# Routed experts in pairs and singles of 128 rows, one three-buffer ring for both weights, and two reordered attention loops

## What is computed

```python
scores = sigmoid(flat @ centroids.T) + bias          # 16 routed experts
vals, idx = top_k(scores, 4)                         # 4 of them for every row
gating = zeros_like(scores).at[rows, idx].set(vals); gating /= gating.sum(-1)
for w1, b1, w2, b2, g in routed experts:             # D 512, hidden 352 (padded to 384)
    acc += (relu(flat @ w1 + b1) @ w2 + b2) * g[:, None]
```

## Time and profile before

| what | value |
|---|---|
| runs | 2126.97 us median of 3 (2122.52 to 2127.93) |
| the profiled execution | 2123.35 us, its span 2121.6 us |
| PE, DVE, ACT, POOL busy | 85%, 58%, 40%, 49% |
| granted TensorE clock, mean | 0.92 |
| DMA, mean | 149 GB/s |

### The profile page before, as it was taken

How to read it: one execution, slowest core, us unless ns; L and a number is a source line. 1 busy time by engine, 2 the same in 40 slices (tenths; PEclk the granted TensorE clock), 3 DMA queues, 4 the chain that set the end, 5 groups by cost and what they waited for, 6 DMA issues and landing times. The chain is left out here.

```text
span 2121.6 us, 29604 instructions
## 1 busy us (share of the span) xinstructions
PE 1803.0 (85%) x10016; PEld 1475.2 (70%) x10016; DVE 1231.4 (58%) x1916; ACT 848.3 (40%) x1426; POOL 1032.3 (49%) x654
## 2 busy tenths in 40 slices
PE   3389999999999688986669956765999999996996
PEld 2189999999999333432238845655999999995775
DVE  5244544444444579999606623662666666565886
ACT  3233333433333246455321211442666666661221
POOL 0325453545454245554312566213877777764564
PEclk7699999999999899998879977877999999998998
DMA  5634232323333400221680141103788778776564
GB/s 204 213 115 135 90 120 101 109 100 119 104 110 124 175 20 26 94 90 59 208 314 1 41 169 29 47 1 109 269 284 286 276 281 282 274 258 206 195 205 132
DMA packets 106858, 316.86 MB, mean 149 GB/s; under 512 B 14531, under 2 KB 16161, under 8 KB 105505
## 3 DMA queue, kind: packets, MB, share of 16 engines
q1 hardware_dynamic: 89536, 266.07, 36.5%
q0 software_dynamic: 17248, 49.86, 7.0%
HBM read 248.17 MB, written 67.71 MB: 149 GB/s over the span
## 5 line engine op out<-in xcount | busy, mean ns | idle before, releaser
L703 DVE TENSOR_TENSOR rffn_ps_h<-rffn_ps_hidden,rffn_silu 128x256 f32<-128x256 f32 x128 | 55.4, 432 | 234.3 <-ACT rffn_silu L658 234.3
L692 DVE TENSOR_TENSOR rows<-rffn_ps_y,rows 128x512 f32<-128x512 f32 x255 | 165.1, 681 | 2.5 <-PE rffn_ps_y L766 1.1
L745 PE MATMUL rffn_ps_hidden<-rffn_xsh,rffn_w0h 128*128 128x256 f32 x512 | 147.7, 288 | 0.0
L745 PE MATMUL rffn_ps_hidden<-rffn_xsl,rffn_w0h 128*128 128x256 f32 x512 | 146.0, 285 | 0.0
L745 PE MATMUL rffn_ps_hidden<-rffn_xsh,rffn_w0l 128*128 128x256 f32 x512 | 145.9, 285 | 0.0
L658 ACT ACTIVATE rffn_silu<-rffn_ps_hidden 128x256 f32<-128x256 f32 x144 | 53.3, 370 | 230.0 <-PE rffn_ps_hidden L745 226.6
L621 POOL TENSOR_TENSOR rffn_w0l<-rffn_raw,rffn_w0h 128x1536 fp32r<-128x1536 f32 x15 | 52.7, 3513 | 177.6 <-ACT rffn_w0h L642 177.6
L1873 POOL DMA_INDIRECT moe_x_in<-xn_rows,moe_idx_now x94 | 99.4, 1057 | 21.2 <-issue 14.7
L1879 POOL TENSOR_TENSOR moe_w_0l<-moe_raw,moe_w_0h 128x1536 fp32r<-128x1536 f32 x24 | 84.3, 3514 | 40.2 <-ACT moe_w_0h L1904 40.2
L745 PEld LDWEIGHTS rffn_ps_hidden<-rffn_xsh,rffn_w0h 128*128 128x128 f32 x512 | 99.2, 194 | 3.6 <-issue 0.3
L745 PEld LDWEIGHTS rffn_ps_hidden<-rffn_xsl,rffn_w0h 128*128 128x128 f32 x512 | 99.3, 194 | 1.8
(11 more groups left out here) (710 smaller groups left out, 6352.5 us busy)
## 6 DMA issues: line engine op xcount, KB each, us to landing
rffn_raw<-in_ffn_w SPq DMA_DIRECT2D x80, 768.0 KB, 4.3
moe_raw<-in_moe_w SPq DMA_DIRECT2D x47, 769.5 KB, 4.3
moe_raw<-in_moe_w SPq DMA_DIRECT2D x47, 768.0 KB, 5.2
ys<-moe_y SPq DMA_DIRECT2D x47, 512.0 KB, 3.0
xs<-route_zero SPq DMA_DIRECT2D x17, 256.0 KB
rffn_x_in<-xs SPq DMA_DIRECT2D x17, 256.0 KB, 2.7
ys<-rows SPq DMA_DIRECT2D x17, 256.0 KB, 2.1
rows<-in_x SPq DMA_DIRECT2D x4, 1024.0 KB, 9.0
```

The costliest lines, as they stand in the source:

```text
L692: nc.vector.tensor_tensor(y[:, 2 * u + tt, :], yb[n % 2][tt][:], y[:, 2 * u + tt, :], ALU.add)\
L703: nc.vector.tensor_tensor(hp[:, n % 2, :], hb[n % 2][:, 1, :], sil[n % 2][:], ALU.mult)\
L745: last = nc.tensor.matmul(hb[n % 2][:, half, :], wu[p][:, col:col + P], xs[q][:, c, u * PR:(u + 1) * PR], start=(c == 0 and m == 0), stop= ...
```

## The change

The routed experts' rows are now padded to 128, not 256. Every expert has full tiles of 256 rows (a pair of 128) and, where 128 rows or fewer are left, a single of 128. There are `MP` = 31 pairs and `MS` = 17 singles, 48 units in place of 47 tiles, in the fixed order 2, 2, 1, fourteen times, then 2, 1, three times; the units of a kind take the experts' rows in turn, and `places` and `shares` compute the places and experts of both kinds. A single does the same weight work and half of everything else. w1 and w2 share a ring of three buffers: load number q = 2m + second goes to buffer q % 3. POOL gathers for unit m + 2 before it subtracts for m + 1. ACT casts the first hidden parts before the last relu. In the window attention `exps` and `shift` of step u + 1 come ahead of the splitting of step u; in the stream `scores` is cut in two, its first part ahead of `turn_p`.

```diff
-MT = T * 4 // MR + 15
+MP, MS = 31, 17
+MU = MP + MS
+MG = 2 * MP + MS
...
+MKINDS = [2, 2, 1] * 14 + [2, 1] * 3
...
-        raw1 = [a.sb(f"raw1_{j}", [P, W1 + MF]) for j in range(2)]
-        raw2 = a.sb("raw2", [P, W2])
+        raw = [a.sb(f"raw{k}", [P, W1 + MF]) for k in range(3)]
...
+        def ring(m, second):
+
+            return (2 * m + second) % 3
...
-                if after(s, 2):
-                    src = weights_of(A["moe_w1"], s + 2)
-                    wait(sp, s_w1, s + 1)
-                    sp.dma_start(raw1[j][:], src).then_inc(s_raw1[j], 16)
-                if after(s, 1):
-                    src = weights_of(A["moe_w2"], s + 1)
-                    wait(sp, s_w2, s + 1)
-                    sp.dma_start(raw2[:], src).then_inc(s_raw2, 16)
+            def load(i, m, second):
+                k = ring(m, second)
+                src = weights_of(A["moe_w2"] if second else A["moe_w1"], i, m)
+                if not (isinstance(i, int) and 2 * (MCYC * i + m) + second < 3):
+                    if second:
+                        sp.wait_ge(s_w1, number(i, m))
+                    else:
+                        sp.wait_ge(s_w2, number(i, m) - 1)
+                sp.dma_start(raw[k][:, 0:W2 if second else W1 + MF], src).then_inc(s_raw[k], 16)
...
+            def run(i, m):
+                if exists(i, m + 1):
+                    load(i, m + 1, 1)
+                if exists(i, m + 2):
+                    load(i, m + 2, 0)
+                if not at_start(i, m):
+                    store(i, m - 1)
...
-                if after(s, 1):
-                    split(s + 1, 1 - j)
-                if after(s, 2):
-                    gather(s + 2, j)
+                if exists(i, m + 2):
+                    gather(i, m + 2)
+                if exists(i, m + 1):
+                    split(i, m + 1)
...
             for u in range(2 * HKV):
-                exps(u)
-                if u:
-                    probs_high(u - 1)
                 probs(u)
+                if u + 1 < 2 * HKV:
+                    exps(u + 1)
+                probs_high(u)
...
             for u in range(2 * HKV):
-                shift(u)
+                inverse(u)
+                if u + 1 < 2 * HKV:
+                    shift(u + 1)
                 if u:
                     probs_low(u - 1)
-                inverse(u)
...
             for u in range(2 * HKV):
-                turn(u)
                 if u + 2 < 2 * HKV:
                     scores(u + 2)
+                turn(u)
...
                 if 0 <= n - 1 < NR:
                     turn_q(n - 1)
+                if 0 <= n - 1 < NR:
+                    scores(n - 1)
                 if 0 <= n - 2 < NR:
                     turn_p(n - 2)
                 if 0 <= n - 1 < NR:
-                    scores(n - 1)
+                    geo_scores(n - 1)
```

More of the change, by code:

```diff
@@ new lines, in _, with store @@
+            load(0, 0, 0)
+            load(0, 0, 1)
+            load(0, 1, 0)
+            def run(i, m):
[5 more added lines that the diff above has]
+                    store(i, m - 1)
+            def store(i, m):
+                n = kind(i, m)
+                first = tile_no(i, m)
+                dst = ys_dram[some(first * P, n * P), :]
+                wait(sp, s_yc, tiles_ahead(i, m) + n)
+                sp.dma_start(dst.rearrange("(t p) d -> p t d", p=P), y[:, 0:n]).then_inc(s_out, 16)
@@ L1910, in _, with run, relu @@
             split1(0, 0)
             high_x(0, 0)
-            def run(s, j):
-                if after(s, 1):
-                    split1(s + 1, 1 - j)
-                wait(act, s_raw2, 16 * (s + 1))
-                wait(act, s_y, 2 * (s - 1))
-                nc.scalar.copy(w2[j][HI][:], raw2[:]).then_inc(s_w2hi, 1)
-                for f in range(MF):
+            def run(i, m):
+                j, n, s = m % 2, kind(i, m) * P, number(i, m)
+                if exists(i, m + 1):
+                    split1(i, m + 1)
+                wait(act, s_raw[ring(m, 1)], loads(i, m, 1))
+                if not at_start(i, m):
+                    wait(act, s_y, tiles_ahead(i, m - 1))
+                nc.scalar.copy(w2[j][HI][:], raw[ring(m, 1)][:, 0:W2]).then_inc(s_w2hi, 1)
+                def relu(f):
@@ L1949, in _, with run, low_h @@
             low_x(0, 0)
[L1951 removed]
+            def run(i, m):
+                j, n, s = m % 2, kind(i, m) * P, number(i, m)
                 wait(dve, s_w2hi, s + 1)
[L1953 to L1954 removed]
+                nc.vector.tensor_tensor(w2[j][LO][:], raw[ring(m, 1)][:, 0:W2], f32(w2[j][HI][:]), ALU.subtract)\
+                  .then_inc(s_w2, 1)
+                def low_h(f):
@@ L1963, in _, with turn_x @@
-            copy_y(MT - 1)
+                low_h(0)
+                low_h(1)
+                if exists(i, m + 1):
+                    low_x(i, m + 1)
+                low_h(2)
+                if not at_start(i, m):
+                    copy_y(i, m - 1)
+            units(dve, run)
+            copy_y(MU // MCYC - 2, 2 * MCYC - 1)
         @block.tensor
         def _(pe):
-            def turn_x(s, j):
-                for tt in range(2):
+            def turn_x(i, m):
+                j = m % 2
+                for tt in range(kind(i, m)):
```

279 lines of the change are left out of this document (160 added, 119 removed).

## The result

The changed kernel takes 2228.4 us (median of 4 runs, 2226.0 to 2229.0) against 2124.7 of the kernel before: ratio 1.049, 95% interval 1.047 to 1.050. The forecast was 2210 us, range 2185 to 2248. The profiled execution took 2228.2 us, its span is 2226.1 us.

A forecast was written before the change was run, and what follows sets the result against it. The prediction took PE as the routed experts' bound before and a closed loop of w1 loads after. Stage +101.6, router +3, window -12, stream -6 sum to +86.6 on the profiled 2123.35: 2210 us, range 2185 to 2248.

The forecast's parts named there:

- The loop, the mechanism: Routed experts: each w1 load waits for the one before through ACT, DVE and SP, once per unit; stage +101.6 us.
- The signs that the prediction named: Routed experts' profile: ACT's load waits over 150 us, w2 subtraction 3.7 to 3.8, DMA some 215 GB/s, PE some 75%.
- Its size: Routed experts, one turn of the loop: 6.95 plus 4.4 for the load, 11.35 us; 47 intervals 533.5 us.
- The 3.8 us: Routed experts: DVE's subtraction of w2 stands still during POOL's subtraction, taking 3.8 us, against 1.76 alone.
- PE's hidden products on 128 columns: Routed experts, singles: 36 hidden products on half the columns save nothing, 36 x 0.11 = 4.0 us.
- The 39 us for the units: Routed experts: 48 units take PE 399 us against 438, 39 us less, if PE remains the bound.
- The stage's end: Routed experts, after the last hidden product's start: 10.4 us in place of 12.8.
- rival 3: Routed experts: PE's idle time in the loop drops its clock to 1.2 GHz every third unit, +48 us, 2258; chance 0.16.
- Rival 2: Routed experts: the loop never closes, PE bounds, the stage is 39 us shorter, total 2069 us; chance 0.06.
- Router: Router: new small operations before the first list of places add 3 us, bounds +2 and +6.
- Window: Window attention: next step's `shift` and `exps` fill DVE's 1.98 us hole per step; -12 us, bounds -20 and +5.
- Stream: Stream: first scores run while DVE and ACT make probabilities, 14 rounds x 0.45; -6 us, bounds -9 and +2.

The follow-up runs named there:

- e1: Changed kernel with ACT's cast of w2 moved ahead of the bias copy and w1 cast of the next unit: 2114.7 us, ratio 0.997.
- e11: Changed kernel with ACT casting w1 twice in every unit, the second time after the first is done: 2295.3 us, ratio 1.081.
- e2: Changed kernel with one more wait: POOL subtracts w1 of the next unit only after DVE's subtraction of w2: 2177.3 us, ratio 1.027.
- e3: Changed kernel, pairs and singles kept, with the buffers and SP's load order of the kernel before: 2097.0 us, ratio 0.989.
- e5: e1 with DVE's subtractions for x of the next unit ahead of those for hidden: 2094.1 us, ratio 0.985.
- e10: Changed kernel with POOL's order of before, gathers behind the subtraction of w1 again: 2224.2 us, ratio 1.048.
- e12: e5 with POOL's residual addition first in the stream, and ACT casting w1 twice in every unit: 2124.9 us, ratio 1.001.
- e4: Kernel before with only the change's two attention orders, window and stream: 2111.8 us, ratio 0.995.
- e7: e4 with POOL's addition of the residual ahead of its rotated-query addition and gathers in the stream: 2106.9 us, ratio 0.992.

## Why the prediction was right, step by step

- **The loop, the mechanism:** as worked out. "Every load of w1 waits for the one before it, through ACT, DVE and SP" is what the turn above shows; e1 opens it (-114 us), e11 lengthens it (+66.9), e2 shortens one term of it (-51). The signs that the prediction named came out for ACT's wait (253 us for loads, over 150 forecast), w2's subtraction, SP's issue 0.17 us behind it and the DMA engines' 211 GB/s (215 forecast). PE's share did not: 83%, not 75%, since the forecast counted its products at full clock.
- **Its size:** forecast 6.95 + 4.4 = 11.35, measured 6.95 + 4.53 = 11.48 a turn (4.42 to landing and 0.11 until ACT starts); 47 intervals 533.5 forecast, 535.1 measured, since the first two (9.3 and 9.2) run on loads made before the loop closes. The two errors are +6 us (46 turns by 0.13) and -4; that they nearly cancel is luck.
- **The 3.8 us:** forecast 3.7 to 3.8, measured 3.79 (47 of 48; the last, with no subtraction of POOL left, 1.75). e2 shows the 2.03 us of exclusion in it. The Trainium skill (SBUF — State Buffer, Who interferes with whom) says that the two contend when DVE reads two SBUF inputs and POOL reads SBUF, and the trace agrees for w2, for the hidden sums (3.25 us for two in e1) and for att_p (2.18 us). That the one that issues first blocks the other agrees for w2 and for the hidden sums of e1, not for att_p, where DVE's record starts first and DVE is held. The prediction looked for the exclusion only at w2. Its remark that by this rule the gain of the narrower y work could not show does not follow: y's copy reads PSUM, and what hid the gain was the loop.
- **PE's hidden products on 128 columns:** 0.110 to 0.114 each in a row at the full clock (middle half of 483), as taken from the earlier trace rows. The 39 us for the units are confirmed in part: 47 undisturbed distances of e3 (8.4 on average) and its end of 10.6 would make a stage of 405 us, 37 under the one before; with e3's long distances 22 were measured.
- **The stage's end:** forecast 10.4 us after the last unit's start, measured 13.7; the granted clock was 0.5 (1.2 GHz) from 2012.3 to 2019.1 there. In e3 and e5, where it was not, 10.6 and 10.5; in e1, e2, e10 and e12, where it fell in the same place, 13.7 to 13.8. This is the step of rival 3, in miniature: 3 us.
- **Rival 3** in the stage: the clock did fall, to 0.90 on average, with 22 stretches at 1.2 GHz between those at 2.4, but no turn of the loop was longer for it: in none of the 45 did a term other than the load vary by more than 0.14 us. The waits for loads covered it, as argued. The Trainium skill (TensorE: Matmul & The Clock Gate, HAM oscillation) describes a loop of bursts and waits in which every burst starts cold; the trace agrees in part, with 22 such stretches in 47 distances. Inside the stage they cost nothing, because PE was not the bound. Rival 2's time needed e5's edit besides the open loop, and the 2069 us were not reached (2094).
- **Router:** forecast +3. The first window instruction comes at 1322.5 on average in the three profiles without the new operations (1321.8 to 1323.9) and 1325.6 in the eleven with them (1322.6 to 1329.4): +3, give or take about 1.
- **Window: the term that was mis-sized.** Forecast -12, measured -3.5 from the first `win_` instruction to the first hidden product (-4.2 in e4). The steps did shrink, from 7.18 to 5.12 us, DVE's bound: first to last reciprocal 57.7 to 47.0. But I priced the steps and not what they feed: attend(2) and attend(3) on PE, at 1.2 GHz in part, end the stage, and PE was no earlier with them. From the last reciprocal to the first product after them it was 9.3 us before, 15.1 after.
- **Stream: mis-sized too.** Forecast 0.45 a round and -6; measured 0.10 and -2.0 (-4.5 in e4). DVE's wait left as said; POOL's addition took its place. Both terms stayed inside the bounds given for them, but these errors, and not the loop, make most of the 18 us.

The 18 us between 2210 and 2228 are 9 from the start (router +3 and window -12 against -0.1), 4 from the stream, 3 from the stage's end, 2 from the turns.

## What to carry to other kernels

When buffers of several loads are shared, write down for each load the chain that frees its buffer and go on until you meet a load again: if it is the previous load of the same kind, the period is that chain's sum, however idle the engines on it look, and exchanging two instructions on one of them can be worth more than the buffers. Sharing buffers moved the wait here and removed none; ask which instruction stands ahead of the freeing one on its engine. When a wait on DVE goes, look at what POOL will now run beside it.

## What was not expected of the hardware

- A 770 KB load landed in 4.1 to 4.8 us when the load before it was down, and in 5.9 us on average when that had 2.6 us or more to go (e2): so a shorter loop paid back nearly half of its gain (0.87 of 2.03 us) as longer loads. I read this as two loads sharing the DMA engines; no run separates it from other causes.
- The exclusion of DVE and POOL also hits in small places: 128 x 512 with one broadcast input (0.69 us alone, 2.18 beside a 1.31 us addition, although DVE's record starts first), and POOL's copy of a unit's row numbers, 1 or 2 columns: 0.19 us with DVE idle, 1.6 to 1.74 in 43 of 48 units of the changed kernel, as at 1755.70, where it starts under DVE's subtraction and ends with it. It did so in 38 of 47 tiles of the kernel before as well. DVE's work with one input in PSUM kept its 0.68 us beside POOL's addition (e7, 2003.79 to 2005).
